# A decoder block on one core: how the heads' values reach the output projection, where the row biases are added, and in which order the next batch's projections run

## The reference, cut to what matters

```python
x = _layernorm(x + _L0_attn_ref(x, ...), axis=-1)              # q, k from latents and rope; out @ Wo_w + Wo_b
x = _layernorm(x + _L0_xattn_ref(x, ctx_1024, ctx_1024, mask, ...), axis=-1)   # ... x @ W3.T + b3
x = _layernorm(x + _L0_ffn_ref(x, choice_w, w1, w2), axis=-1)  # top-k routing, two products, scatter-add
# in both attentions, for each of the 16 heads:
#   p = softmax(q k^T * scale);  head = p @ v;  heads joined to 256 columns, then the output projection
#   v = (latent or context) @ Wv + bv
```

## Time and profile before

| | |
|---|---|
| median of three runs | 1955.38 us |
| lowest and highest | 1953.38, 1956.86 us |
| profiled execution, its own time | 1959.72 us |
| its span | 1957.9 us |
| PE, DVE, ACT, POOL busy | 1668.1, 1134.5, 891.8, 429.8 us |
| stretch from self to cross, batches 0, 1, 2 | 71.9, 72.1, 71.3 us |
| the same for batch 3 (nothing of a next batch) | 57.7 us |
| cross-attention, batches 0 to 3 | 75.4, 75.6, 76.6, 60.9 us |
| stretch from cross to self, batches 0, 1, 2 | 33.2, 33.1, 33.1 us |
| the same for batch 3 | 32.1 us |
| self-attention, batches 1, 2, 3 | 200.4, 201.1, 196.6 us |

### The profile page before, as it was taken

One profiled execution on the slowest core, in us unless ns is written; L12 is line 12 of the kernel. 1 busy time (PEld: TensorE's weight loads), 2 busy tenths in 40 slices (PEclk: granted clock), 3 DMA queues, 4 the chain that ended last, 5 costly groups with the idle time before them and its releaser, 6 DMA issues. The chain is left out here.

```text
span 1957.9 us, 32981 instructions
## 1 busy us (share of the span) xinstructions
PE 1668.1 (85%) x10632; PEld 848.3 (43%) x10632; DVE 1134.5 (58%) x1939; ACT 891.8 (46%) x1585; POOL 429.8 (22%) x547
## 2 busy tenths in 40 slices
PE   6599988798999888989998798999967844999993
PEld 3033334444332445433324354333245433888883
DVE  5577725756777256567763665677435366333424
ACT  2077773342777534347774343577833300111112
POOL 5200004302000052020001611100031001555563
PEclk9599999897999988979998899799988955999997
DMA  6700003622000044220000632200003040335446
GB/s 187 163 2 1 2 25 87 163 48 71 2 2 2 27 127 134 49 59 2 2 2 27 164 98 53 54 2 2 2 21 78 2 150 28 75 77 107 77 89 193
DMA packets 98037, 120.07 MB, mean 61 GB/s; under 512 B 17180, under 2 KB 73500, under 8 KB 97820
## 3 DMA queue, kind: packets, MB, share of 16 engines
q1 hardware_dynamic: 85468, 97.13, 18.1%
q0 software_dynamic: 12416, 20.98, 5.7%
HBM read 80.30 MB, written 40.79 MB: 62 GB/s over the span
## 5 line engine op out<-in xcount | busy, mean ns | idle before, releaser
L881 ACT ACTIVATE pT<-banks 128x512 f32<-128x512 f32 x1184 | 645.2, 596 | 254.8 <-PE banks L1492 150.0
L1034 DVE TENSOR_REDUCE nmf<-banks 128x1 f32<-128x1024 f32 x512 | 606.0, 1220 | 173.5 <-PE banks L1442 171.6
L1492 PE MATMUL banks<-qst,kst 99*128 99x512 bf16 x1024 | 344.0, 388 | 12.1 <-DVE nmf L1034 6.3
L1442 PE MATMUL banks<-kst,qst 96*128 96x512 bf16 x1024 | 327.0, 404 | 31.9 <-DMA kst<-k_parts 21.8
L1524 PE MATMUL banks<-pT,V 128*32 128x512 f32 x2048 | 273.8, 606 | 20.6 <-ACT oT L872 14.0
L1492 PEld LDWEIGHTS banks<-qst,kst 99*128 99x128 bf16 x1024 | 96.0, 97 | 307.2 <-ACT pT L881 185.8
L703 POOL CAST nmp<-nmf 128x16 bf16<-128x16 f32 x64 | 12.7, 198 | 831.4 <-DVE nmf L1034 516.6
L944 ACT ACTIVATE kst<-banks 128x512 f32<-128x512 f32 x64 | 38.2, 597 | 287.0 <-PE banks L1747 278.6
L1442 PEld LDWEIGHTS banks<-kst,qst 96*128 96x128 bf16 x1024 | 98.6, 100 | 146.4 <-DVE nmf L1034 37.3
L1029 DVE TENSOR_REDUCE nmf<-banks 128x4 f32<-128x616 f32 x128 | 99.6, 797 | 86.6 <-PE banks L1436 79.7
L1053 DVE RECIPROCAL rz<-banks 128x16 f32<-128x16 f32 x64 | 16.1, 251 | 204.5 <-PE banks L1552 203.4
(11 more groups left out here) (176 smaller groups left out, 2016.7 us busy)
## 6 DMA issues: line engine op xcount, KB each, us to landing
qst<-q_parts SPq DMA_DIRECT2D x48, 256.0 KB, 5.2
kst<-k_parts SPq DMA_DIRECT2D x48, 256.0 KB, 3.8
qst<-in_w SPq DMA_DIRECT2D x16, 512.0 KB
q_parts<-kst SPq DMA_DIRECT2D x48, 128.0 KB, 2.5
k_parts<-kst SPq DMA_DIRECT2D x48, 128.0 KB, 3.9
qx_parts<-kst SPq DMA_DIRECT2D x48, 128.0 KB, 3.1
qxs<-qx_parts SPq DMA_DIRECT2D x24, 256.0 KB, 5.0
qst<-qx_parts SPq DMA_DIRECT2D x24, 256.0 KB, 4.9
```

The source lines that it names most:

```text
L881: act.activation(pT[:, n % RING_P, :], PS[:, banks[what, n], :], ACT.Exp, scale=scale).then_inc(s_ex, 1)
L1034: dve.tensor_reduce(nmf[:, m % 2, j, t:t + 1], scores.rearrange("p a n -> p (a n)"), AX.X, ALU.max, negate=True).then_inc(s_smu, 1)
L1442: ins = pe.matmul(pair[:, half, :], qst[0:KQ, h, t * P:(t + 1) * P], kst[0:KQ, h, half * N:(half + 1) * N], start=True, stop=True)
L1492: ins = pe.matmul(ps, kst[0:KM, head, kc * P:(kc + 1) * P], qst[0:KM, head, cols], start=True, stop=True)
```

## The change

- `o_tiles`, `turn_heads` and `heads_out` go. ScalarE copies a group's bank to one of only two slots, `avr` (the old `oT` is gone). SP moves it on by 8 small DMAs a group (`compact`): four put the rows of sums into a 128x128 tile `sums`, four put the 16 rows of values of each head and half to their place in `xT`. In the self-attention group g - 2 is moved behind the loads of group g's maxima; in the cross-attention group g - 4, and the last four groups behind the last load.
- VectorE takes one reciprocal of `sums` (128x128). TensorE spreads the inverses over the heads' rows by 16 float32 products with the constant 0/1 matrices `spread` (`inverses`), and VectorE multiplies `xT` by the four banks (`divided`).
- The row biases: `bias_parts` makes bv @ Wo + bo once at the start, in three bf16 parts. `output` adds it by one more product of 96 rows for each tile of 128 tokens. The broadcast adds on GpSimd go, and the additions of the values' biases on VectorE become copies; those of the self-attention move to ScalarE (`values`).
- Order. TensorE makes the latents before the inverses, and the values and the first half of q between the output projection and the turns of the layer norm; the other half of q comes behind `qx`. The context's keys and values move ahead of the inverses of the cross-attention.
- `xT` of the next batch has a buffer of its own (`xTf`) and is loaded early. The pieces 9 to 12 use other slots of `pT`. The first normalised result is kept in `xb`, which is the residual of the next sum.

The group of maxima made ahead (`ahead`) stands in both versions.

```diff
-FRONT = LATENTS + OPERANDS + CONTEXT
-OUT_SELF = [("o", "D")] * T + [("oT", "DA"[n % 2]) for n in range(4)] + [("y", "D")] * 4
+FRONT = LATENTS + HALF_Q * 2 + KEYS + VALUES + CONTEXT
+OUT_SELF = [("bc", "D")] * 4 + [("y", "D")] * 4
-EACH = Plan(OUT_SELF + LATENTS + INTO_CROSS + OPERANDS, OUT_CROSS + CONTEXT + ROUTING)
+EACH = Plan(LATENTS + OUT_SELF + VALUES + HALF_Q + INTO_CROSS + HALF_Q + KEYS, CONTEXT + OUT_CROSS + ROUTING)
...
+            def compact(b, cross, g):
+
+                wait_apart(sp, s_ave, b * 2 * NG + (NG if cross else 0) + g + 1)
+                slot = avr[:, g % 2, :]
+                for k in range(N // P):
+                    sp.dma_start(sums[4 * g + k:P:V32, :], slot[HD:P:V32, k * P:(k + 1) * P]).then_inc(s_oc[g % 2], 16)
+                for j in range(TILES):
+                    (h, half), rows = (g * G + j // HALVES, j % HALVES), slice(V32 * j, V32 * j + HD)
+                    sp.dma_start(xT[h % 8 * HD:(h % 8 + 1) * HD, h // 8, half * N:(half + 1) * N],
+                                 slot[rows, :]).then_inc(s_oc[g % 2], 16)
...
-                    act.activation(oT[:, k, :], PS[:, AV_BANK, :], ACT.Copy).then_inc(s_ave, 1)
+                    act.wait_ge(s_oc[k % 2], 128 * (b * NG + (NG // 2 if n0 else 0) + k // 2) + START)
+                    act.activation(avr[:, k % 2, :], PS[:, AV_BANK, :], ACT.Copy).then_inc(s_ave, 1)
...
+            def divided(at, b, name, cross):
+
+                for i in range(2):
+                    dve.wait_ge(s_oc[i], 128 * (b * NG + (NG if cross else NG // 2)) + START)
+                dve.reciprocal(sums[:, :], sums[:, :]).then_inc(s_rz, 1)
+                for n in range(4):
+                    idx, (half, c) = at.nth(name, n), divmod(n, 2)
+                    cols = slice(half * N, (half + 1) * N)
                     ready(at, idx)
+                    dve.tensor_tensor(xT[:, c, cols], xT[:, c, cols], PS[:, at.bank(idx), :],
+                                      ALU.mult).then_inc(s_evd, 1)
...
+            def inverses(at, b, name, cross):
+
+                pe.wait_ge(s_rz, b * 2 + (2 if cross else 1))
+                for n in range(4):
+                    half, c = divmod(n, 2)
+                    ps = item(at, at.nth(name, n))
+                    for k in range(N // P):
+                        ins = pe.matmul(ps[:, k * P:(k + 1) * P], spread[:, c, half, k, :], sums[:, :],
+                                        start=True, stop=True)
                     ins.then_inc(s_item, 1)
...
+                        pe.matmul(tile, onesb[0:3 * V32, :], bias3[:, row, :], start=True, stop=False)
                         for c in range(C):
-                            ins = pe.matmul(ps[:, (t % 2) * D:(t % 2 + 1) * D], xT[:, c, t * P:(t + 1) * P],
-                                            w[:, c, :], start=(c == 0), stop=(c == C - 1))
+                            ins = pe.matmul(tile, xT[:, c, t * P:(t + 1) * P], w[:, c, :], start=False, stop=(c == C - 1))
...
             def rest_of_batch(b, more):
                 at = Place(EACH if more else LAST, b)
-                o_tiles(at, "o", 0, T)
-                turn_heads(at, "o", "oT")
-                output(at, "oT", "y", wo)
                 if more:
                     latents(at, b + 1)
+                inverses(at, b, "bc", False)
+                output(at, "bc", "y", wo, 0)
+                if more:
+                    values(at)
+                    operands(at, "q", 0)
                 turn_normalised(at, b, "x1T", 0)
...
                 if more:
-                    for name in "qk":
-                        for half in range(HALVES):
-                            operands(at, name, half)
-                    values(at)
+                    operands(at, "q", 1)
+                    operands(at, "k", 0)
+                    operands(at, "k", 1)
```

More of the change, by code:

```diff
@@ L260, in decoder_block @@
         pT = sb("pT", [P, RING_P, N])
-        full, rest = pT[:, 4:6, :], pT[:, 6:8, :]
+        full = [pT[:, 4 + i % 2 if i < 9 else (i - 9) % 2, :] for i in range(PIECES)]
+        rest = [pT[:, 6 + i % 2 if i < 9 else 2 + (i - 9) % 2, :] for i in range(PIECES)]
         ctkv = sb("ctkv", [P, S])
@@ L544, in self_attention @@
                     load_minus_max(b, g, qst[:, g * G:(g + 1) * G, :])
+                    if g >= 2:
+                        compact(b, False, g - 2)
             def cross_rows(g):
@@ L551, in rest_of_batch @@
                     load_x(b + 1)
+                for g in range(NG - 2, NG):
+                    compact(b, False, g)
                 wait_apart(sp, s_qx[0], b * 96, s_qx[1], b * 96, s_ql[1], b * 96 + 96)
@@ L670, in _ @@
             link(pool.memset(Vr[:, :, HD:HD + 1], 1.0))
+            link(pool.memset(bias3[:, :, :], 0.0))
+            link(pool.memset(spread[:, :, :, :, :], 0.0))
+            for c, half, k in itertools.product(range(C), range(HALVES), range(N // P)):
+                link(pool.affine_select(out=spread[:, c, half, k, :], in_=spread[:, c, half, k, :],
+                                        compare_op=ALU.not_equal, fill=1.0, base=-(V32 * half + HD * c + k),
+                                        pattern=[[-4, NG // 2], [-2 * V32, G], [0, HD]], channel_multiplier=1))
             link(pool.memset(kxst[:, :, :], 1.0))
```

260 lines of the change are left out of this document (126 added, 134 removed).

## The result

| | before | after |
|---|---|---|
| device us, median (range) | 1954.53 (1953.38 to 1956.86) | 1999.19 (1989.36 to 2004.59) |
| ratio of after to before, 95% interval | | 1.0221 (1.018 to 1.0262) |
| profiled execution: own time, span | 1959.72, 1957.9 | 1998.61, 1996.8 |

The change costs 2.2%. The loops of the attentions are nearly untouched, and the time went where heads become a residual sum. I cut both traces at the same events: the end of the last copy of values of an attention, the first product of the next attention's maxima.

A forecast was written before the change was run, and what follows sets the result against it. It took the eight stretches between attentions, lines of dependent steps, as deciding the change's worth. Terms 8.1 + 31.6 + 5.2 = 44.9 us on the 1955.4 median gave 2000.3, stated as 2000; range 1970 to 2016.

The forecast's parts named there:

- The queue (a): End of cross-attention: SP's queue of small DMAs delays group 7, landing at 443.2 after a copy ending at 434.25.
- Reciprocal, 0.9: VectorE's reciprocal of the 128x128 sums, after the transfers: 0.9 us, taken along the slope of two rows.
- Products, 4.2 at the full and 6.2 at the low clock: The 16 float32 products with `spread` before the projection: 4.2 us at full clock, 6.2 us after an idle wait.
- rival 1: Dear products with `spread`: 0.22 us an instruction at either clock, 7.0 us in all, giving 2012; chance 0.15.
- From cross to self, 7.9 four times: Stretches behind the four cross-attentions: 8.1 later projection, plus 0.3 for bias, less 0.5 for context; 31.6 us in all.
- (d): Cross to self, context ahead: VectorE's two copies leave the gap between normalised half and its turns, -0.5 us.
- From self to cross, 2.7 three times and 5.2: Cross-attention starts 2.7 us later in batches 0 to 2 (8.1 in all) and 5.2 later in batch 3.
- sign of being wrong: Wrong if group 7's DMAs start early, VectorE's rope starts the cross-attention, or attentions change by over 1 us each.
- Batch 3, 4.95 for the projection: Batch 3, self to cross: nothing fills the wait for transfers, so the projection starts 4.95 us later.
- (b): Bias by TensorE: eight more products a stretch, 0.3 us on VectorE's chain; the work removed from GpSimd counted as nothing.
- (e): Added waits in the attentions, for ScalarE's slots and SP's `compact`, and set-up at the start: cost nothing.
- Rival 3: Faster: SP issues tiny DMAs in 0.36 us or less, group 7 lands by 438; some 5 us off, 1950; chance 0.09.

The follow-up runs named there:

- one_dma: The changed kernel with the four small transfers of a group's sums made one, five transfers a group instead of eight; 1.0100 of before.
- a_wait: The changed kernel with TensorE, ahead of the cross-attention's q products, waiting only for the ScalarE copies it reads, not VectorE's rope; 1.0164 of before.
- h_bias: The kernel before with row biases on TensorE, no residual sum on GpSimd, values copied by ScalarE behind the cross-attention's q, heads as before; 0.9984 of before.
- h_fold: The kernel before with values copied by ScalarE behind the cross-attention's q, their biases folded in once, output biases still on GpSimd; 0.9951 of before.
- h_dve: The kernel before with row biases on TensorE and no residual sum on GpSimd, values copied by VectorE and last as before; 1.0020 of before.
- a_nobias: The changed kernel without the row-bias products ahead of each tile of the output projections; 1.0216 of before.
- a_late: The changed kernel with one transfer for a group's sums, clock-keeping products, values and half of q behind the cross-attention's q, latents still ahead; 1.0030 of before.
- a_swap: The same kernel as a_late, but with the latents behind the output projection again; 0.9990 of before.
- a_order: The changed kernel with TensorE's old order between a batch's attentions: latents, first half of q and values moved back, values last; 1.0273 of before.
- one_wait: The changed kernel with both one transfer for a group's sums and TensorE's wait for ScalarE's copies alone; 1.0063 of before.

## Why the prediction was right, step by step

Predicted 2000.0, measured 1999.19; 44.9 us more by the sum, 44.7 by the medians and 45.8 by the cuts. The mechanism was the one named, and one_dma showed it: the queue alone is over half of the loss. That the numbers meet within 1 us is partly luck. The cuts have 27.9 us from cross to self for 31.6, and against that 2.4 in the cross-attentions, 1.9 at the start and 0.3 from self to cross that the sum had not. The terms:

- *The queue (a).* Predicted: last landing 9.0 us behind the copy, reciprocal done at 9.95. Measured 9.90 (8.95 + 0.95). Right: group 7's transfers began 2.8 us behind the copy, 2.3 predicted, and from there it took 6.1 us to the reciprocal, 6.7 predicted.
- *Reciprocal, 0.9.* It took 0.95 everywhere. The slope of two rows held up to 128 columns. The Trainium skill ("VectorE: DVE Perf Modes", First, the fixed hardware budget) says that a reciprocal divides by iteration with a repeat count of 8. It gives no time; the 6.3 ns a column from 16 columns (251 ns) to 128 (952) don't contradict it.
- *Products, 4.2 at the full and 6.2 at the low clock.* 3.73 and 5.5 to 6.7 (6.67, 5.65, 6.26 and 6.06 behind the four cross-attentions). 0.117 an instruction at the full clock, so 0.13 was a little high; rival 1 is out by a factor of two. The Trainium skill ("TensorE: Matmul & The Clock Gate", LDWEIGHTS) has one formula for a load, without the clock in it, which gives 107 ns for 128 columns. The 0.117 at the full clock come near, but the price was 0.208 at a granted clock of 0.50 to 0.64: here it follows the clock.
- *From cross to self, 7.9 four times.* 7.27, 6.26, 6.70 and 7.7: 27.9 for 31.6. The projection came 16.6, 15.6 and 16.0 us behind the copy (16.2 predicted). What was off is (d): I credited 0.5 us less 0.3 for the context ahead. From the projection to the self-attention it took 25.1 before and 23.9 after, so 1.2 us were won; the context's products left TensorE's line, not VectorE's alone. Batch 3 has no context, so the sum's 0.5 was credited there without a reason: behind its projection (15.3 us behind the copy, 8.1 before) it lost 0.5.
- *From self to cross, 2.7 three times and 5.2.* 4.61, 1.09, 4.06 and 3.79: 13.6 for 13.3. The sum is right by two errors. The turns were 4.5, 3.2 and 4.5 us later (5.4 predicted), but from the turns to the stored parts it took 4.6, 2.4 and 4.1 us more, by TensorE's wait for the rope and, in batches 0 and 2, the low clock behind it (missed; a_wait showed it). Behind the stored parts the stretch was 4.5 shorter in each (365.74 - 347.97 against 358.77 - 336.46 in batch 0) where I had counted the values' 2.7 alone. All of the 4.5 comes with the values' move: h_bias and h_fold, which make nothing ahead of the turns, have 17.8 to 17.9 us there, as after has. With the values as copies on VectorE (h_dve) it is 20.2. The cross-attention's first product waits for VectorE's rope, which was named as a sign of being wrong, but that rope hangs on the stored parts: the way from them is 17.77 us in all three batches.
- *Batch 3, 4.95 for the projection.* 3.67 (12.64 - 8.97): the reciprocal came 6.20 us behind the copy (6.7 predicted), and the products took 5.49.
- *(b), 0.3 a projection and nothing for GpSimd.* a_nobias shows some 0.7 in a stretch from cross to self by the cuts and nothing that the medians can tell, and batch 3 has 0.5 behind its projection. A little more than predicted.
- *(e), nothing.* Wrong by 2.4 us in the cross-attentions; cross-attention 1, at 1.09, passes the 1 us that was named as a sign of being wrong. The waits for a slot made the last copy 1.2 us later in batches 0 and 1; batches 2 and 3 have none. The working had group 5's transfers start with their copy and found group 7's slot free just in time. They started 2.45 us later (435.30 for 432.85), because group 4's were still being issued: these eight took 7.5 us (427.70 to 435.20) in place of 5.1, since the first two took 1.57 and 2.16. The 9.4 us for a group was also an average; the copies are 7.8 to 2.9 us apart. one_dma took the slot waits back.
- *Rival 3, faster at 3.6 us to the last landing.* one_dma had 4.8 us to the reciprocal's start and was still 1.0% slower than before, as the other costs stood. The working of this rival was also 1 us short: 0.36 us an issue from 434.3 on and a landing of 2.2 give 439.0, not 438.

## What to carry to other kernels

A row of small transfers costs the engine that issues it some 0.6 us each, for 2 KB (0.55) as for 32 KB (0.61). Count the issues behind the last producer, and make them one transfer with more dimensions before reordering anything. A wait that covers a whole list of items grows when an item is moved ahead of it: wait for the engine that wrote what is read. What is put ahead as cover has to be weighed against the wait that it covers: with short transfers the latents ahead cost 0.4% (a_late against a_swap), and no run shows that they paid with the long ones. A run that moves an order back should move one thing, or its trace has to say which of them cost (a_order's loss stands at the values). An addition that stands on an idle engine (GpSimd's biases) was not saved here by moving it to the busiest one; a gain such as the values' move should be tried alone, without what came with it.

## What the runs showed of the hardware that I had not expected

- A pause of 2.48 us on TensorE was followed by 3.8 us at a granted clock of 0.58 (8.71 us for the 16 products), and in batch 1 a pause of 2.47 us by the same products in 7.13. Behind the same 2.42 us pause at the end of cross-attention 0, one_dma has the small products at 5.47 us and one_wait at 3.84. The rows don't show what tells them apart.
- Behind ten useless products and a pause of 1.72 us the clock was still full: 3.84 us for the 32 products, for 6.66 behind a pause of 6.59.
- One transfer of 8 KB with three dimensions was issued in 0.58 us, like one of 2 KB with two dimensions (four in 2.19 by the queue's row); merging four cost nothing, and the reciprocal stayed 1.45 us behind the last issue.
- The self-attentions of batches 1 to 3 start at a granted clock of 0.50, and how long that lasts makes up to 3 us. In one_dma, 12 us behind the start of the self-attentions of batch 1 (196.7 us in all) and batch 2 (199.2), the same columns as the earlier trace rows:
```profile
484.80:490.80 6.00, 6.00 (x32) 1.77 (x31) 4.82 (x5) 4.32 (x9) 0.00 (x0) 0.91 0.00 0
868.50:874.50 6.00, 6.00 (x19) 1.44 (x18) 2.78 (x3) 2.90 (x6) 0.00 (x0) 0.50 0.00 0
```
  So a gain in a stretch ahead of a self-attention can be taken back, or a loss be made up, without any change there. No run shows what decides it.
